# Two scans of 512 columns joined into one of 1024 in a Mamba-style decoder layer, with the first column of the second state corrected ahead of the scan

## The chip, the cores and the metric

The kernel runs on one core of one Trainium2 chip. A core has four compute engines with a queue of instructions each: PE (TensorE, matmuls; PEld are its weight loads), DVE (VectorE), ACT (ScalarE) and POOL (GpSimd). SP (SyncE) only issues DMAs here. The engines run side by side and wait for one another by semaphores. The metric is the device time of one execution in microseconds (us). The kernel before takes 3095.3 us, the median of three runs (3093.15 to 3097.14).

## The reference, cut to what matters

One decoder layer on x of 2 sequences x 2048 tokens x 512 features, float32: a selective scan (Mamba), a cross attention, a feed-forward part, each followed by a layer norm. The change concerns the selective scan alone:

```
xz = x @ W_in + b_in;  u = silu(first half);  z = second half       # 1024 channels each
B, C = split(u @ W_xproj + b_xproj)                                 # 16 states each
dt = softplus(u @ W_dt + b_dt);  A = -exp(A_log)                    # A: 1024 x 16
for t in time:                                                      # separately per sequence
    h = h * exp(dt[t] * A) + (dt[t] * u[t]) * B[t]                  # h: 1024 x 16
    y[t] = sum over states(h * C[t]) + D * u[t]
out = (y * silu(z)) @ W_out + b_out
```

For one channel and one state this is a recurrence over time, h = decay * h + input. VectorE has an instruction for it, which runs along the columns of a row and takes the value before the first column as a separate operand.

## The kernel before, in words

`selective_scan_phase` fills about the first 1925 us, `attention_ffn_phase`, which the change leaves alone, the rest. The scan phase cuts the 4096 tokens into 8 chunks of 512 (`TS`), four per sequence; the 1024 channels into 8 tiles of 128; and a tile with its 16 states into 8 pairs. A row on the 128 partitions is 8 channels x 16 states of one group, so a pair is two such groups (`o` = 0 and 1) and there are 8 x 8 x 8 = 512 pairs. Each engine goes through the pairs in the same order; what it does in the turn of one pair is called a slot here, and slots count from 0 to 63 within a chunk.

For one pair: PE spreads dt over the states into `r_ps` (`rep_dt`, L400, two banks of 512 columns, twice two matmuls) and dt*u into `u_ps` (`rep_dtu`, L413). ACT makes the decays in place, two `Exp` (`exps`, L642). DVE multiplies `u_ps` by B into the buffer `h` (`dbu`, L786), and scans each of the two rows of `h` with its bank of `r_ps` (`scans`, L799, two instructions), starting from `carry` where the chunk continues a sequence and from zero in chunks 0 and 4. ACT saves the last column of both rows (`save_carry`, L648). POOL multiplies by C (`weigh`, L903), and PE sums over the states into `y_ps` (L429). Per tile, DVE gates y (`gate`, L805) and ACT scales u by D (`skip`, L653).

`r_ps` holds two pairs. So `rep_dt(pair + 2)` waits for the scans of `pair`; after it come `exps(pair + 2)` on ACT, then the scans of `pair + 2` on DVE, which has `dbu(pair + 2)`, the scans of `pair + 1` and `dbu(pair + 3)` to do in between. That is the loop in which the change lies. `s_scan`, `s_da` and `s_m1` count scans, decays and `dbu`.

Beside that, in the slots of chunk n the engines make u, z and dt of chunk n + 1, by a written table (`Plan`): which slots hold which projection on PE, where ACT splits the next x into two float16 parts (`x_high`, `Plan.x`, and `x_low` on POOL, L870), and when the silu of u and z and the softplus of dt run on ACT. A silu brings two loads of an activation table. There are eight silu in a chunk's slots, each of two tiles. In the last chunk the projection by W_out begins from slot 24 on (`OUTS`); its weights are split into float16 parts in slots 15 to 23 (`w_out_high`, `w_out_scaled` on ACT, `w_out_low` on DVE, L810, and on POOL, L925).

SP issues all loads and stores in one order (`step(c, j)`: one call for each chunk and tile), so whatever it waits for holds back what stands behind it.

Of the kernel before, what the change touches and what calls it, by code (L numbers as in the profile page):

```python
# [9 lines left out]
ALU = mybir.AluOpType  # L10
# [45 lines left out]
W_OUT_LOW_AT = (19, 20, 22, 23)  # L56
# [6 lines left out]
class Plan:  # L63
    def __init__(self, n):
# [13 lines left out]
        start = 31 if n == 1 else 26  # L78
        self.x = {1: (25, 28), 2: (20, 23)}.get(n, (19, 23))
        self.u_high = (start + 8, start + 16)  # L80
        at, places = start, {}
        for name in self.order:
            long = name in ("dt3", "dt4", "dt5", "dt6", "dt7") and 2 <= n < NC - 1
# [37 lines left out]
def selective_scan_phase(nc, a):  # L121

    with ExitStack() as ctx:
# [38 lines left out]
        c_rep = sb("c_rep", [P, 2, TS])  # L162
        h = sb("h", [P, H_GROUPS, 4, TS])
# [18 lines left out]
        s_hl = sem("a_last_hc_ready")  # L182
        s_hc, s_sum, s_y, s_skip = sem("a_hc_ready"), sem("a_summed"), sem("a_y_ready"), sem("a_skip_ready")
# [3 lines left out]
        s_wor, s_woh, s_wos, s_wol, s_wod = (sem(f"a_w_out_{n}") for n in ("loaded", "high", "scaled", "low", "first_low"))  # L187
# [25 lines left out]
        x_stages = (x_t, soft)  # L213

        def place(pair):
            return pair // PAIRS, pair % PAIRS // 8, pair % 8

        @block.sync
        def _(sp):
            def load_x(n, part, stage):  # L220
# [83 lines left out]
            def step(c, j):  # L304
                more = c + 1 < NC
                if j == 6 and more:
                    store_z(c + 1, 0)
                load_u(c, j)
                load_z(c, j)
# [8 lines left out]
                if more:  # L318
# [8 lines left out]
                    if j == 7:  # L327
                        store_z(c + 1, 1)

            def load_y_tile(i):  # L330
                g = i % 4
                if i < 2:
                    sp.wait_ge(s_wod, i + 1)
                elif i < 4:
                    sp.wait_ge(s_wol, 2 * i - 2)
# [53 lines left out]
        def _(pe):  # L389
            def rep_dt(pair):  # L390
# [11 lines left out]
                last.then_inc(s_rep, 1)  # L402

# [68 lines left out]

            def out_piece(i, s):
                out = OUTS[i]
                k0, k1 = out.pieces[s]
                if s == out.first:
                    if i == 0:
                        pe.wait_ge(s_ev, pieces_before(NC))
                        pe.wait_ge(s_wod, 2)
# [3 lines left out]
                else:  # L483
                    if i == 0 and k0 == 3:
                        pe.wait_ge(s_wol, 4)
# [34 lines left out]
            for w in range(2):  # L520
                spread_state(first, w, r_ps[:, 2 + w, :])
            rep_dt(0)
            rep_dtu(0)
            pe.wait_ge(s_ev, first.index("C") + 1)
            rep_dt(1)
            rep_dtu(1)
            for pair in range(TOTAL):
# [4 lines left out]
                s = pair - (NC - 1) * PAIRS  # L532
                for i in range(OUT_TILES):
# [10 lines left out]
        def _(act):  # L544
# [64 lines left out]
            def evacuate_dt(plan, t, src=pj[:, :]):  # L609
                g = plan.n * NJ + t  # L610
                act.wait_ge(s_pj, plan.index(f"dt{t}") + 1)
# [24 lines left out]
            def exps(pair):  # L636
                c, j, p = place(pair)
                act.wait_ge(s_rep, pair + 1)
                for o in range(2):
                    col = j * NSTATE + 2 * p + o  # L640
                    bank = r_ps[:, 2 * (pair % 2) + o, :]
                    nc.scalar.activation(bank, bank, ACT.Exp, scale=decay[:, col:col + 1]).then_inc(s_da, 1)  # L642

            def save_carry(pair):
                c, j, p = place(pair)
                act.wait_ge(s_scan, 2 * pair + 2)
# [43 lines left out]

            def w_out_scaled(q):
                act.wait_ge(s_woh, q + 1)
                rows = slice(2 * q, 2 * q + 2)
                nc.scalar.activation(w_out_raw[:, rows, :], w_out_raw[:, rows, :], ACT.Copy, scale=W_SCALE).then_inc(s_wos, 1)
# [52 lines left out]
            for pair in range(TOTAL):  # L747
# [7 lines left out]
                if pair + 2 < TOTAL:  # L755
                    exps(pair + 2)
                if pair % 8 == 3:
# [1368 lines left out]
```

## Time and profile before

| | us |
|---|---|
| median of three runs | 3095.3 |
| the profiled execution's own time | 3097.61 |
| its span, first to last instruction | 3095.9 |
| DVE busy | 2697.2 |
| PE busy | 2835.3 |
| ACT busy | 2008.8 |
| POOL busy | 1827.0 |

The share of busy time mixes two phases; the scan phase is read from windows inside it. The chain that ended last could not be followed far back in this profile: its named parts add up to less than half the span, nearly all of them in the second phase. For the scan phase it is the idle time of DVE, and what ended it, that says what bounds.

### The profile page before, as it was taken

How to read it: one execution, taken by the hardware profiler on the slowest of the kernel's cores; microseconds unless marked ns; L12 is line 12 of the kernel's file. 1: busy time of each engine (PE TensorE's matmuls, PEld its weight loads, DVE VectorE, ACT ScalarE, POOL GpSimd, SP SyncE). 2: the span in 40 equal slices, each digit the busy share in tenths (PEclk: the TensorE clock that was granted, in tenths of full speed). 3: DMA queues.
4: the chain of work that ended last, by engine and by line, in shares of the span. 5: the costliest groups of instructions: out<-in, count | busy, mean ns of one | idle time of the engine just before them, and what ended most of it. 6: DMA issues, size and time to landing. Idle time of an engine off the chain costs nothing. (4 is left out here: it accounts for less than half of the span.)

```text
span 3095.9 us, 48996 instructions
## 1 busy us (share of the span) xinstructions
PE 2835.3 (92%) x18940; PEld 1263.5 (41%) x18940; DVE 2697.2 (87%) x3072; ACT 2008.8 (65%) x3600; POOL 1827.0 (59%) x940
## 2 busy tenths in 40 slices
PE   7988989889889889889899898899999999999998
PEld 2222222222222222222222223566666767667665
DVE  6999999999999999999999988776666777777775
ACT  6777776676776776776777644555555555655565
POOL 4887988888888888888988987312211111111100
PEclk9999999999999999999999899899999999999999
DMA  4112111111111121111122233701111000010000
GB/s 162 52 52 70 42 56 61 52 52 56 52 57 56 46 65 53 41 65 53 42 65 80 87 96 119 233 29 43 43 43 46 33 23 23 23 37 29 23 8 15
DMA packets 123897, 176.65 MB, mean 57 GB/s; under 512 B 15154, under 2 KB 50610, under 8 KB 123156
## 3 DMA queue, kind: packets, MB, share of 16 engines
q1 hardware_dynamic: 123668, 173.51, 17.3%
q8 instruction: 155, 2.54, 0.3%
q14 instruction: 74, 0.61, 0.1%
HBM read 104.33 MB, written 67.04 MB: 55 GB/s over the span
## 5 line engine op out<-in xcount | busy, mean ns | idle before, releaser
L903 POOL TENSOR_TENSOR h<-h,c_rep 128x1024 f32<-128x1024 f32 x511 | 1197.9, 2359 | 242.2 <-ACT carry L648 241.1
L799 DVE TENSOR_TENSOR_SCAN h<-r_ps,carry,h 128x512 f32<-128x512 f32 x768 | 938.6, 1262 | 5.5 <-ACT r_ps L642 5.4
L642 ACT ACTIVATE r_ps<-r_ps,decay 128x512 f32<-128x512 f32 x1024 | 631.8, 656 | 330.1 <-PE r_ps L400 330.0
L786 DVE TENSOR_TENSOR h<-u_ps,b_rep 128x1024 f32<-128x1024 f32 x512 | 612.9, 1197 | 21.7 <-PE u_ps L413 21.6
L413 PE MATMUL u_ps<-dtu,spread 32*128 32x512 f16 x2048 | 313.6, 383 | 115.1 <-DVE h L786 113.5
L400 PE MATMUL r_ps<-dt,spread 32*128 32x512 f16 x2048 | 312.8, 381 | 44.5 <-DVE h L799 44.3
L1989 POOL TENSOR_TENSOR o_in<-o_in,rows 128x1024 f32<-128x1024 f32 x15 | 37.0, 2464 | 487.7 <-DMA o_in<-o_dram 487.7
L799 DVE TENSOR_TENSOR_SCAN h<-r_ps,zero,h 128x512 f32<-128x512 f32 x256 | 312.8, 1261 | 3.6 <-ACT r_ps L642 3.6
L429 PE MATMUL y_ps<-h,gather 128*32 128x512 f32 x2048 | 285.1, 624 | 0.0
L40 PE MATMUL fps<-x,region 128*128 128x256 f16 x1024 | 280.5, 274 | 3.0 <-issue 2.4
L42 PE MATMUL fps<-x,region 128*128 128x256 f16 x1024 | 280.1, 274 | 0.0
L41 PE MATMUL fps<-x,region 128*128 128x256 f16 x1024 | 280.0, 273 | 0.0
L40 PE MATMUL pj<-x_high,region 128*128 128x512 f16 x484 | 190.5, 394 | 41.7 <-POOL x_low L870 18.8
L400 PEld LDWEIGHTS r_ps<-dt,spread 32*128 32x128 f16 x2048 | 59.0, 92 | 378.0 <-DVE h L799 220.8
L2007 POOL TENSOR_TENSOR y<-y_t,y 128x1024 f16<-128x1024 f32 x13 | 29.2, 2248 | 299.1 <-ACT y L1505 299.1
L40 PE MATMUL nat<-region,act 128*128 128x512 f16 x512 | 194.4, 380 | 4.2 <-DVE act L1776 4.2
L40 PE MATMUL pj<-u_high,region 128*128 128x512 f16 x504 | 196.3, 389 | 2.0 <-ACT zs L587 1.3
L41 PE MATMUL pj<-u_low,region 128*128 128x512 f16 x504 | 194.4, 386 | 0.0
L42 PE MATMUL pj<-u_high,region 128*128 128x512 f16 x504 | 194.4, 386 | 0.0
L41 PE MATMUL nat<-region,act 128*128 128x512 f16 x512 | 194.2, 379 | 0.0
L42 PE MATMUL nat<-region,act 128*128 128x512 f16 x512 | 194.2, 379 | 0.0
L42 PE MATMUL pj<-x_high,region 128*128 128x512 f16 x484 | 189.0, 390 | 0.0
(257 smaller groups left out, 5599.3 us busy)
## 6 DMA issues: line engine op xcount, KB each, us to landing
u_t_dram<-u SPq DMA_DIRECT2D x16, 1024.0 KB, 5.1
uz<-u_t_dram SPq DMA_DIRECT2D x64, 256.0 KB, 3.8
z_t_dram<-zs SPq DMA_DIRECT2D x32, 512.0 KB, 3.0
uz<-z_t_dram SPq DMA_DIRECT2D x64, 256.0 KB, 3.6
y_t_dram<-uz SPq DMA_DIRECT2D x64, 256.0 KB, 2.1
region<-y_t_dram SPq DMA_DIRECT2D x32, 256.0 KB, 3.5
result<-x SPq DMA_DIRECT2D x16, 512.0 KB, 2.8
x_t<-dram_x_t SPq DMA_DIRECT2D x15, 512.0 KB, 4.3
```

The source lines that it names most:

```text
L40: nc.tensor.matmul(out, w[0], x[0], start=start, stop=False)
L41: nc.tensor.matmul(out, w[0], x[1], start=False, stop=False)
L42: return nc.tensor.matmul(out, w[1], x[0], start=False, stop=stop)
L400: last = nc.tensor.matmul(r_ps[:, 2 * (pair % 2) + o, :], spread[32 * i:32 * i + 32, p // 2, :], dt16[32 * i:32 * i + 32, s, j, :], start= ...
L413: last = nc.tensor.matmul(u_ps[:, o, :], spread[32 * i:32 * i + 32, p // 2, :], dtu16[32 * i:32 * i + 32, s, j, :], start=(s == 0), stop=( ...
L429: last = nc.tensor.matmul(y_ps[32 * i:32 * i + 32, :], gather[:, q, :], h[:, g % H_GROUPS, i, :], start=(q == 0), stop=(q == 3))
L642: nc.scalar.activation(bank, bank, ACT.Exp, scale=decay[:, col:col + 1]).then_inc(s_da, 1)
L786: nc.vector.tensor_tensor(h[:, g % H_GROUPS, o:o + 2, :], u_ps[:, :, :], b_rep[:, c % 2:c % 2 + 1, :].broadcast_to([P, 2, TS]), ALU.mult). ...
L799: nc.vector.tensor_tensor_scan(row, r_ps[:, 2 * (pair % 2) + o, :], row, start, ALU.mult, ALU.add)\
L903: nc.gpsimd.tensor_tensor(rows, rows, c_rep[:, c % 2:c % 2 + 1, :].broadcast_to([P, 2, TS]), ALU.mult)\
L1989: nc.gpsimd.tensor_tensor(o_in[:, :, :], o_in[:, :, :], row(0), ALU.add).then_inc(s_ob, 1)
L2007: nc.gpsimd.tensor_tensor(y16[:, 1, :, t * P:(t + 1) * P], y_first[i % 2] if i < Y_PAIRED else y_t[:, :, :], y16[:, 0, :, t * P:(t + 1) * ...
```

## The change

Where a chunk continues a sequence, the second row of a pair is now scanned behind the first in the same instruction, 1024 columns from one start. For this the decay in the first column of the second row must be zero, so that nothing runs over from the first row, and what the recurrence would have added there, decay * carry, must already stand in that column of `h`.

- The first columns of banks 1 and 3 of `r_ps` are set to zero once (`joint_decay_zero`). After that `rep_dt` and `exps` leave them out for `o` = 1: 511 columns instead of 512.
- The missing decay is worked out apart. For each tile, SP stores the first column of dt (128 numbers) to DRAM and, once that has landed, loads it back spread over the states (`joint_dt`); POOL multiplies by A (`joint_dt_scaled`), ACT takes `Exp` (`joint_decay`), 8 decays per partition for the 8 pairs.
- For each pair ACT adds decay * carry to the first column of the second row (`joint_column`), after `dbu` of that pair and its `exps`. The scan waits for both `Exp` and for this column.
- All this is done in the six chunks that continue a sequence (1 to 3, 5 to 7); in chunks 0 and 4 the start is zero and only the joined scan is new.
- `evacuate_dt` on ACT also waits until the first column of the tile two before has been stored.
- `Plan`: the production for chunk 1 starts at slot 32 instead of 31, for chunk 2 at 27 instead of 26, with x one slot later for chunk 2; dt3 for chunk 2 takes 3 slots instead of 4. PE waits for the two halves of the split x apart, each where it needs it.
- `step` on SP loads u and z before it stores z, where it did it behind.
- Last chunk: DVE makes all four low parts of W_out (slots 17 to 20), where it made two and POOL the other four half-size pieces after two scalings on ACT. PE runs 6 more matmuls, whose result nobody reads, in each of the slots 21, 22 and 23 (`keep_awake`).

```diff
-        start = 31 if n == 1 else 26
-        self.x = {1: (25, 28), 2: (20, 23)}.get(n, (19, 23))
+        start = {1: 32, 2: 27}.get(n, 26)
+        self.x = {1: (25, 28), 2: (21, 24)}.get(n, (19, 23))
...
+            def joint_dt(n, t):
+                if n >= NC or not continued(n):
+                    return
+                done = joints_before(n) * NJ + t
+                sp.wait_ge(s_dt, n * NJ + t + 1)
+                sp.dma_start(a["dt_first"][n, t, :].rearrange("(c r) -> r c", c=8),
+                             dt[:, (n * NJ + t) % 2, 0:1], allow_slow_non_contiguous=True).then_inc(s_jst, 16)
+                sp.wait_ge(s_jst, 16 * (done + 1))
...
+                sp.dma_start(joint[:, t, :, :, :].rearrange("p h o q -> p (h o q)"), a["dt_first"][n, t, :].rearrange("(c r) -> c r", c=8).unsqueeze(1)
+                             .broadcast_to([8, NSTATE, 16])).then_inc(s_jld[t % 2], 16)
...
-                    pe.wait_ge(s_scan, 2 * pair - 2)
+                    pe.wait_ge(s_scan, pair - 1)
...
-                        last = nc.tensor.matmul(r_ps[:, 2 * (pair % 2) + o, :], spread[32 * i:32 * i + 32, p // 2, :],
-                                                dt16[32 * i:32 * i + 32, s, j, :], start=(s == 0), stop=(s == 1))
+                        last = nc.tensor.matmul(r_ps[:, 2 * (pair % 2) + o, o:TS], spread[32 * i:32 * i + 32, p // 2, :],
+                                                dt16[32 * i:32 * i + 32, s, j, o:TS], start=(s == 0), stop=(s == 1))
...
-                        if s == plan.u[0][0]:
-                            pe.wait_ge(s_xl, 2 * n + 2)
+                        if t == 0:
+                            pe.wait_ge(s_xl, 2 * n + 1 + plan.u[0].index(s))
...
+            def keep_awake():
+                pe.wait_ge(s_ev, pieces_before(NC))
+                for k in range(6):
+                    nc.tensor.matmul(pj[:, :], w_out[0][:, 0, 0:P], w_out[0][:, 0, :], start=True, stop=True)
...
-                    bank = r_ps[:, 2 * (pair % 2) + o, :]
+                    bank = r_ps[:, 2 * (pair % 2) + o, o:TS]
                     nc.scalar.activation(bank, bank, ACT.Exp, scale=decay[:, col:col + 1]).then_inc(s_da, 1)
...
+            def joint_column(pair):
+                c, j, p = place(pair)
+                if continued(c):
+                    if p == 0:
+                        act.wait_ge(s_jexp, joints_before(c) * NJ + j + 1)
+                    act.wait_ge(s_m1, pair + 1)
+                    act.wait_ge(s_carry, pair - PAIRS + 1)
+                    col = j * NSTATE + 2 * p + 1
+                    at = h[:, pair // 2 % H_GROUPS, 2 * (pair % 2) + 1, 0:1]
+                    nc.scalar.activation(at, joint[:, j, p % 2, 1, p // 2:p // 2 + 1], ACT.Identity, bias=at, scale=carry[:, col:col + 1])\
+                        .then_inc(s_joint, 1)
...
                 if pair + 2 < TOTAL:
+                    joint_decay(pair + 2)
                     exps(pair + 2)
+                    joint_column(pair + 2)
...
-                for o in range(2):
-                    col = j * NSTATE + 2 * p + o
-                    dve.wait_ge(s_da, 2 * pair + o + 1)
-                    row = h[:, pair // 2 % H_GROUPS, 2 * (pair % 2) + o, :]
-                    start = carry[:, col:col + 1] if c % PER_SEQ else zero[:, 0:1]
-                    nc.vector.tensor_tensor_scan(row, r_ps[:, 2 * (pair % 2) + o, :], row, start, ALU.mult, ALU.add)\
-                        .then_inc(s_scan, 1)
+                dve.wait_ge(s_da, 2 * pair + 2)
+                if continued(c):
+                    dve.wait_ge(s_joint, joints_before(c) * PAIRS + pair % PAIRS + 1)
+                o = 2 * (pair % 2)
+                col = j * NSTATE + 2 * p
+                rows = h[:, pair // 2 % H_GROUPS, o:o + 2, :].rearrange("p o t -> p (o t)")
+                start = carry[:, col:col + 1] if continued(c) else zero[:, 0:1]
+                nc.vector.tensor_tensor_scan(rows, r_ps[:, o:o + 2, :].rearrange("p o t -> p (o t)"), rows, start,
+                                             ALU.mult, ALU.add).then_inc(s_scan, 1)
...
-                if W_OUT_AT + 2 <= s < W_OUT_AT + 4:
+                if W_OUT_AT + 2 <= s < W_OUT_AT + 6:
                     w_out_low(s - W_OUT_AT - 2)
```

ACT's queue in chunk 3, slots 6 and 7 at the start of tile 1's decays (`carry` begins a slot's work on the loop; L592 is the silu of z with its table loads, L633 and L634 split dt), before:

```order
955 L587 ACTIVATE zs<-pj,b_in 128x512 [waits a_projected]
956 L648 ACTIVATE carry<-h 128x2 [waits a_scanned]
957 L642 ACTIVATE r_ps<-r_ps,decay 128x512 [waits a_dt_spread]
958 L642 ACTIVATE r_ps<-r_ps,decay 128x512
959 L592 ACT_TABLE_LOAD
960 L592 ACTIVATE zs<-zs 128x1024 [waits a_evacuated]
961 L546 ACT_TABLE_LOAD
962 L648 ACTIVATE carry<-h 128x2 [waits a_scanned]
963 L642 ACTIVATE r_ps<-r_ps,decay 128x512 [waits a_dt_spread]
964 L642 ACTIVATE r_ps<-r_ps,decay 128x512
```

and now, at the same place (L721 is `save_carry`, L697 `exps`, L714 `joint_column`, L703 `joint_decay`, L644 the silu):

```order
1108 L721 ACTIVATE carry<-h 128x2 [waits a_scanned]
1109 L697 ACTIVATE r_ps<-r_ps,decay 128x512 [waits a_dt_spread]
1110 L697 ACTIVATE r_ps<-r_ps,decay 128x511
1111 L714 ACTIVATE h<-joint,h,carry 128x1 [waits a_carry_saved,a_dbu_ready]
1112 L644 ACT_TABLE_LOAD
1113 L644 ACTIVATE zs<-zs 128x1024 [waits a_evacuated]
1114 L598 ACT_TABLE_LOAD
1115 L721 ACTIVATE carry<-h 128x2 [waits a_scanned]
1116 L703 ACTIVATE joint<-joint 128x2x4 [waits a_joint_dt_scaled]
1117 L697 ACTIVATE r_ps<-r_ps,decay 128x512 [waits a_dt_spread]
1118 L697 ACTIVATE r_ps<-r_ps,decay 128x511
1119 L714 ACTIVATE h<-joint,h,carry 128x1 [waits a_carry_saved,a_dbu_ready,a_joint_decay_ready]
```

The `Exp` stay where they were; behind each pair's two stands a column of one element per partition, and ahead of a tile's first pair the small `Exp` of its eight decays.

DVE's queue in the last chunk, slots 16 to 19 (L810 is `w_out_low`), before:

```order
1002 L786 TENSOR_TENSOR h<-u_ps,b_rep 128x1024
1003 L799 SCALAR_TENSOR_TENSOR h<-r_ps,carry,h 128x512 x2
1004 L810 SCALAR_TENSOR_TENSOR region<-region 128x2x512
1005 L786 TENSOR_TENSOR h<-u_ps,b_rep 128x1024
1006 L799 SCALAR_TENSOR_TENSOR h<-r_ps,carry,h 128x512 x2
1007 L810 SCALAR_TENSOR_TENSOR region<-region 128x2x512
1008 L786 TENSOR_TENSOR h<-u_ps,b_rep 128x1024
1009 L799 SCALAR_TENSOR_TENSOR h<-r_ps,carry,h 128x512 x2
1010 L786 TENSOR_TENSOR h<-u_ps,b_rep 128x1024
1011 L799 SCALAR_TENSOR_TENSOR h<-r_ps,carry,h 128x512 x2
1012 L805 TENSOR_TENSOR uz<-y_ps,uz 128x512
```

and now (L854 is `dbu`, L869 the scan, L880 `w_out_low`, L875 the gate):

```order
1002 L854 TENSOR_TENSOR h<-u_ps,b_rep 128x1024
1003 L869 SCALAR_TENSOR_TENSOR h<-r_ps,carry,h 128x1024
1004 L880 SCALAR_TENSOR_TENSOR region<-region 128x2x512
1005 L854 TENSOR_TENSOR h<-u_ps,b_rep 128x1024
1006 L869 SCALAR_TENSOR_TENSOR h<-r_ps,carry,h 128x1024
1007 L880 SCALAR_TENSOR_TENSOR region<-region 128x2x512
1008 L854 TENSOR_TENSOR h<-u_ps,b_rep 128x1024
1009 L869 SCALAR_TENSOR_TENSOR h<-r_ps,carry,h 128x1024
1010 L880 SCALAR_TENSOR_TENSOR region<-region 128x2x512
1011 L854 TENSOR_TENSOR h<-u_ps,b_rep 128x1024
1012 L869 SCALAR_TENSOR_TENSOR h<-r_ps,carry,h 128x1024
1013 L880 SCALAR_TENSOR_TENSOR region<-region 128x2x512
```

Two rows of scans of 512 columns became one of 1024, and two more `w_out_low` stand between the pairs.

## Rows read from the trace of the kernel before

**Rows 1.** The page's first line.

```profile
span 3095.9 us, 48996 instructions
```

**Rows 2.** Windows: stretch, its length, busy us (instructions) per engine, PE clock, DMA share, GB/s.

```profile
1000.00:1200.00 200.00, 177.57 (x1043) 48.88 (x1043) 199.40 (x176) 144.29 (x259) 173.78 (x89) 0.98 0.17 52
```

**Rows 3.** DVE's waits in chunk 4 (987 to 1215 us): total us, times, longest.

```profile
DVE h L799 <- ACT r_ps L642: 0.6, 1, 0.6
```

**Rows 4.** Groups of 400 to 1700 us: form, count, busy us, mean ns, idle before, releaser.

```profile
L799 DVE TENSOR_TENSOR_SCAN h<-r_ps,carry,h 128x512 f32<-128x512 f32 x600 | 733.3, 1262 | 4.3 <-ACT r_ps L642 4.3
L642 ACT ACTIVATE r_ps<-r_ps,decay 128x512 f32<-128x512 f32 x729 | 449.7, 655 | 202.7 <-PE r_ps L400 202.7
L786 DVE TENSOR_TENSOR h<-u_ps,b_rep 128x1024 f32<-128x1024 f32 x364 | 435.4, 1196 | 4.0 <-PE u_ps L413 4.0
...
L805 DVE TENSOR_TENSOR uz<-y_ps,uz 128x512 f32<-128x512 f32 x46 | 30.4, 660 | 0.0
```

**Rows 5.** Timeline, chunk 3, ACT and DVE around three silu: start, us, what, [idle].

```profile
781.16 1.24 ACT L642 ACTIVATE r_ps<-r_ps,decay 128x512 f32<-128x512 f32 x2 [1.61 <-PE r_ps L400]
...
782.42 1.28 ACT L592 ACT_TABLE_LOAD   x1
782.77 2.44 DVE L799 TENSOR_TENSOR_SCAN h<-r_ps,carry,h 128x512 f32<-128x512 f32 x2
...
785.14 1.20 DVE L786 TENSOR_TENSOR h<-u_ps,b_rep 128x1024 f32<-128x1024 f32 x1
...
786.08 0.20 ACT L648 ACTIVATE carry<-h 128x2 f32<-128x2 f32 x1
786.19 1.22 ACT L642 ACTIVATE r_ps<-r_ps,decay 128x512 f32<-128x512 f32 x2
...
786.96 2.46 DVE L799 TENSOR_TENSOR_SCAN h<-r_ps,carry,h 128x512 f32<-128x512 f32 x2 [0.63 <-ACT r_ps L642]
...
827.65 1.22 ACT L642 ACTIVATE r_ps<-r_ps,decay 128x512 f32<-128x512 f32 x2
...
829.35 2.44 DVE L799 TENSOR_TENSOR_SCAN h<-r_ps,carry,h 128x512 f32<-128x512 f32 x2
...
975.43 1.22 ACT L642 ACTIVATE r_ps<-r_ps,decay 128x512 f32<-128x512 f32 x2
976.33 2.44 DVE L799 TENSOR_TENSOR_SCAN h<-r_ps,carry,h 128x512 f32<-128x512 f32 x2
```

**Rows 6.** DVE's waits in the last chunk (1673 to 1930 us).

```profile
DVE h L786 <- PE u_ps L413: 9.4, 9, 4.6
DVE region L817 <- PE pj L496: 7.0, 2, 4.5
```

**Rows 7.** DMA issues: count, KB each, median us from issue to landing.

```profile
bc_dram<-bc SPq DMA_DIRECT2D x7, 64.0 KB, 1.9
```

**Rows 8.** Timeline, PE before the first u of chunk 1 and of chunk 2.

```profile
179.12 0.61 PE L40 MATMUL pj<-x_high,region 128*128 128x512 f16 x1 [5.71 <-POOL x_low L870]
...
396.26 0.61 PE L40 MATMUL pj<-x_high,region 128*128 128x512 f16 x1 [5.39 <-POOL x_low L870]
```

**Rows 9.** DVE's waits in chunk 0 (57 to 297), then in chunk 1 (297 to 530).

```profile
DVE h L786 <- PE u_ps L413: 6.7, 4, 5.6
...
DVE h L786 <- PE u_ps L413: 3.8, 1, 3.8
```

**Rows 10.** Timeline, last chunk: `w_out_low` on DVE, a POOL one, PE's first output tile.

```profile
1735.99 2.94 DVE L810 SCALAR_TENSOR_TENSOR region<-region 128x1024 f16<-128x1024 f32 x1
...
1737.81 2.14 POOL L890 TENSOR_TENSOR dt<-dt 128x512 f16<-128x512 f32 x1
...
1742.36 2.10 DVE L810 SCALAR_TENSOR_TENSOR region<-region 128x1024 f16<-128x1024 f32 x1
...
1760.14 1.16 POOL L890 TENSOR_TENSOR dt<-dt 128x512 f16<-128x512 f32 x1
...
1769.66 0.58 PE L40 MATMUL pj<-region,u_high 128*128 128x512 f16 x1 [3.61 <-POOL u_low L931]
```

More of the change, by code:

```diff
@@ L82, in __init__ @@
         for name in self.order:
-            long = name in ("dt3", "dt4", "dt5", "dt6", "dt7") and 2 <= n < NC - 1
+            long = name in ("dt4", "dt5", "dt6", "dt7") and 2 <= n < NC - 1 or name == "dt3" and 3 <= n < NC - 1
             count = 2 if name[0] in "uz" else 4 if long else 3
@@ L186, in selective_scan_phase @@
         s_yout = [sem("a_y_stored_even"), sem("a_y_stored_odd")]
-        s_wor, s_woh, s_wos, s_wol, s_wod = (sem(f"a_w_out_{n}") for n in ("loaded", "high", "scaled", "low", "first_low"))
+        s_wor, s_woh, s_wol = (sem(f"a_w_out_{n}") for n in ("loaded", "high", "low"))
         s_bcst, s_brep, s_crep = sem("a_bc_stored"), sem("a_b_replicated"), sem("a_c_replicated")
@@ L305, in step @@
                 more = c + 1 < NC
+                load_u(c, j)
+                load_z(c, j)
+                if j == 7:
+                    joint_dt(c + 1, 0)
+                if j == 1:
+                    joint_dt(c, 3)
+                if j == 2 and c == 1:
+                    joint_dt(c, 4)
                 if j == 6 and more:
                     store_z(c + 1, 0)
-                load_u(c, j)
-                load_z(c, j)
                 if j == 0 and more:
@@ L328, in step @@
                         store_z(c + 1, 1)
+                        joint_dt(c + 1, 1)
+                if j == 0:
+                    joint_dt(c, 2)
+                if j == 1 and c != 1:
+                    joint_dt(c, 4)
+                if j == 2:
+                    joint_dt(c, 5)
+                if j == 3:
+                    joint_dt(c, 6)
+                    joint_dt(c, 7)
             def load_y_tile(i):
                 g = i % 4
[L332 to L335, printed above, removed]
+                if i < 4:
+                    sp.wait_ge(s_wol, i + 1)
                 else:
@@ L532, in _ @@
                 s = pair - (NC - 1) * PAIRS
+                if PLANS[-1].dt[-1][-1] - PAIRS < s < OUT_AT:
+                    if s == PLANS[-1].dt[-1][-1] - PAIRS + 1:
+                        pe.wait_ge(s_woh, 1)
+                    keep_awake()
                 for i in range(OUT_TILES):
@@ L904, in weigh, with joint_dt_scaled @@
                     .then_inc(s_hc, 1)
+            def joint_dt_scaled(pair):
+                c, j, p = place(pair)
+                if continued(c) and p == 0:
+                    pool.wait_ge(s_jld[j % 2], 16 * ((joints_before(c) * NJ + j) // 2 + 1))
+                    odd = decay[:, j * NSTATE:(j + 1) * NSTATE].rearrange("p (q h o) -> p h q o", q=QUADS, h=2)[:, :, :, 1]
+                    nc.gpsimd.tensor_tensor(joint[:, j, :, 1, :], joint[:, j, :, 1, :], odd, ALU.mult).then_inc(s_jmul, 1)
             def produce(plan, s):
@@ L966, in _ @@
                     weigh(pair)
+                if pair + 5 < TOTAL:
+                    joint_dt_scaled(pair + 5)
                 for plan, s in producing(pair):
@@ L969, in _ @@
                 s = pair - (NC - 1) * PAIRS
-                if s in W_OUT_LOW_AT:
-                    w_out_low(4 + W_OUT_LOW_AT.index(s))
                 for i in range(OUT_TILES):
```

46 lines of the change are left out of this document (30 added, 16 removed).

## The prediction

> **What bounds the kernel now.** I read the page first: the span is 3095.9 us [rows 1], the execution's own time 3097.6, 2.3 above the median of the runs, so a sum made on this profile is taken off the median. Then the windows. In a window in the middle of the scan phase DVE is busy 199.4 of 200 us, PE 177.6, POOL 173.8, ACT 144.3, and PE's granted clock is 0.98 [rows 2]. DVE's own waits say the same: in the whole of chunk 4, 228 us long, it waited 0.6 us, once, for ACT [rows 3]. So away from its ends the phase is DVE's queue, and whatever shortens that queue shortens the phase until another engine hands over too late. The reader should keep both halves: DVE has no idle time, and ACT, which hands it the decays, has 28% of slack on average but not in every slot.
>
> **The joined scan.** It removes 512 starts of an instruction. What one start costs I take from two ordinary DVE operations: 512 columns last 660 ns, 1024 columns 1196 [rows 4], so 512 more columns cost 536 and 124 are fixed. A scan of 512 columns lasts 1262; if it takes twice as long per column it spends 2 x 536 = 1072 on columns and 190 on the rest, and one of 1024 would last 2144 + 190 = 2334 ns. The two of before last 2.44 us from the first's start to the second's end [rows 5]. The gain is 0.107 us per pair. The bounds: nothing, if all of the 1262 grows with the columns; 0.19, if the whole rest is saved and none of it overlapped before. I take 0.107, since the count of two per column fits the plain operations' slope. On DVE's path lie 448 pairs of chunks 0 to 6 and 24 of chunk 7: 472 x 0.107 = 50.5 us. In the last 40 pairs the output projection shares PE and DVE already waits for PE [rows 6]; I count half, 2 us. Together 52.5 off.
>
> The Trainium skill ("Perfetto Trace Analysis", Optimizing Scalar/DVE Operations) gives a VectorE instruction on PSUM some 125 ns of overhead and advises larger operations on a saturated engine; by that estimate the term would be 59 us instead of 50.5. The same section says that breaking up instructions can let work be done sooner where an engine holds up others; that is the other side of this change, and the next term.
>
> **What the scan now waits for.** Before, the first scan needed the first `Exp` only: where ACT is late it began 0.13 us after that one's end (786.96, against 786.19 and half of the two) [rows 5]. Now it needs both, and in six chunks a column behind them. A small ACT operation: `save_carry` lasts 0.20 and the next starts 0.11 after it (786.08, 786.19) [rows 5]. The next operation starts about 0.09 before the second `Exp` ends (two of 655 ns in 1.22 us) [rows 4, 5], so the column is ready 0.11 after that end and the scan can begin 0.24 after it; without a column 0.13. Each earlier column also puts ACT 0.11 back. On the other side DVE comes sooner, by 0.107 per scan it did since.
>
> Most pairs have room: ACT has the decays well before DVE comes. It has none behind a silu, whose table loads hold ACT from 782.42 to 786.08, longer than a pair [rows 5]. Eight silu stand in a chunk's slots. Three kinds, all shown [rows 5]:
> - DVE waits already (786.96, idle 0.63). The second `Exp` ends at 787.41, the scan could begin at 787.76 (0.24, and 0.11 of the column before): 0.80 later than now. DVE would have come 0.21 earlier (two scans), which the first term has counted as won. Loss 1.0. There are one or two of these in a chunk; I take two.
> - The five others: `Exp` end 828.87, scan at 829.35. Ready at 829.22, DVE there at 829.14: loss 0.1.
> - Behind a gate: `Exp` end 976.65, scan 976.33. Ready 977.00, DVE there at 976.12: loss 0.9. One per chunk.
> That is 2.0 + 0.5 + 0.9 = 3.4 per chunk, 20 us in six chunks. The `Exp` of eight decays ahead of a tile's first pair, another 0.11, falls on four of these silu: 2.5 us more. In chunks 0 and 4, without columns, 0.79 x 2 + 0.66 = 2.2 each, 4.5. In all 27 us back. Bounds: 10 if only the pairs that wait today lose and the others catch up; 60 if a column is ready 0.5 us later than I reckon, since then all eight silu pairs lose it too (8 x 0.5 x 6 = 24) and pairs with a slack of near 1 us begin to.
>
> **SP, DRAM and POOL.** 48 times SP stores 128 numbers, waits for the landing and loads them. A store of this kind lands in 1.9 us [rows 7], so each holds SP for some 2.5 us, and the value is there some 5 us after dt. The calls stand one to two pairs behind the slot in which dt is made, and POOL wants the value in slot -5 of the tile: 2 pairs of margin for tile 0, over 4 for the rest; in chunk 1 POOL will wait for tile 0's once, some 3 us, and POOL has 26 us in 200 to spare [rows 2]. I count nothing; bound 5 us. If that cover went, POOL's products would come late for PE's sums, then DVE for buffer space.
>
> **The wait for x.** In chunks 0 and 1 PE waited 5.71 and 5.39 us for the second half of the split x [rows 8], and DVE then 5.6 and 3.8 for PE [rows 9]. Now the first projection starts a slot later and its first half needs only the first half of x; a slot is 3.5 us and the second half another, so the wait is gone but for a rest that DVE doesn't see. 9 off; bounds 5 and 9.4.
>
> **The last chunk.** DVE gets two more `w_out_low`: 2.10 us alone, 2.94 where POOL works beside it [rows 10]: 4 to 6 us added. Off go DVE's waits of 4.6 for the first output tile, which PE began 3.61 late because POOL was late, and at half clock [rows 10], and parts of the 7.0 at the first two tiles' ends [rows 6]: POOL is relieved of its `w_out_low`, and `keep_awake` fills PE's idle slots ahead. I take 8 of these 11.6; the ends of the tiles stay on the path. Net 3 off; bounds 4 on, 8 off.
>
> On the two added `w_out_low` the Trainium skill ("SBUF — State Buffer", Who interferes with whom) says that a VectorE instruction with two inputs in SBUF contends with GpSimd's reads. The rows bear it out: beside the L810 of 2.94 us a POOL operation of 1.16 took 2.14 [rows 10]. By that rule both new ones cost 2.9 and POOL 1 us each; by the short row 2.1. I took the middle.
>
> **Sum.** -52.5 + 27 - 9 - 3 = -37.5. From the median, 3095.3 - 37.5 = 3057.8; I say 3057.
>
> **Rivals.**
> 1. The handover becomes the loop. Place: between `exps` on ACT and DVE's scan. If the column reaches DVE 1.2 us after the second `Exp` and not 0.24, the eight silu pairs of a chunk lose 0.96 more and six with a slack of near 1 us some 0.4: 10 us per chunk, 60 in six. 3057 + 60 = 3117, slower. It decides from about 0.85 us on, where the loss eats the 37.5. For it: ACT's bursts are longer than a pair. Against it: a small ACT operation lasts 0.20 [rows 5].
> 2. The joined scan saves nothing, every ns of it growing with the columns. Then DVE also comes no earlier and the second term falls to some 18: 3095.3 + 18 - 12 = 3101. For it: nothing in the trace shows a scan of another length. Against it: 190 ns would be hard to spread over columns that cost twice the plain 536.
> 3. The losses behind the silu are smaller, since a pair that is late gives ACT, PE and POOL time, and PE's clock falls less; the last chunk gains its 8: 3095.3 - 52.5 + 10 - 9 - 8 = 3036.
>
> **Chances.** Forecast (3040 to 3075) 0.58; rival 3 (below 3040) 0.17; between forecast and no change (3075 to 3089) 0.08; rival 1 0.10, of which 0.08 slower and 0.02 no change; rival 2 0.07, half no change, half slower. About 6 us, 0.2%, is what a measurement tells from no change. Faster 0.83, same 0.06, slower 0.11. The range 3030 to 3090 leaves out most of rivals 1 and 2 and the low tail of rival 3, under 0.2 together.
>
> **What the profile after would show.** The scan's row: 512 of them, near 2334 ns; much above 2400 and rival 2 holds. DVE's waits for ACT in a chunk: near 4 us, on some eight pairs, all behind a silu; over 10 and it is rival 1. The column's row near 200 ns. No wait for `x_low` of over 2 us. DVE's waits for PE and for the output tiles in the last chunk: some 8 us instead of 16. Wrong would be: DVE waiting for a loaded dt or POOL's product, a slower matmul of 511 columns, or a span of the second phase that differs.

## The result and the profile after

The changed kernel takes 3122.2 us (median of five runs, 3113.6 to 3124.0) against 3096.6 of before on the same chip: a ratio of 1.0074, 95% interval 1.0062 to 1.0086. It is 26 us slower by the medians, 23 by the ratio; 3057 was forecast. Two of its five runs took 3113.6 and 3113.7, three 3122.2 to 3124.0, so a difference to after is known to some 5 us. The profiled execution is one of 3122.2 us with a span of 3120.2.

The page of after, its first line and the rows of the scan: line, engine, form and count, then busy us and mean ns of one, then the idle time before them and what ended most of it.

```profile
span 3120.2 us, 49910 instructions
...
L869 DVE TENSOR_TENSOR_SCAN h<-r_ps,carry,h 128x1024 f32<-128x1024 f32 x384 | 900.4, 2345 | 54.8 <-ACT h L714 35.2
...
L869 DVE TENSOR_TENSOR_SCAN h<-r_ps,zero,h 128x1024 f32<-128x1024 f32 x128 | 300.9, 2351 | 12.7 <-ACT r_ps L697 12.5
```

The joined scan lasts 2345 ns where 2334 were worked out, against 2.44 us for the two of [rows 5]. But 54.8 us of waiting stand before those of the six continued chunks. The page puts 35.2 down to the column (L714), and 18.7 more, in the row below, to `save_carry` (L721), which stands behind it:

```profile
DVE h L869 <- ACT carry L721: 18.7, 21, 3.3
```

These were waits for the column too: all 21 of these scans start 0.13 us after a column's end, as 52 of the 54 behind L714 do. Two rows say what the column and the decays' `Exp` last (min, median, max in ns), and one how long a store of dt's first column takes to land (count, KB, us):

```profile
L714 ACT ACTIVATE h<-joint,h,carry x384: 377/383/419, 303.1 to 1940.6; 128x1 f32<-128x1 f32 x192
L703 ACT ACTIVATE joint<-joint x48: 191/193/226, 301.9 to 1912.2; 128x8 f32<-128x8 f32 x48
```

```profile
dt_first_dram<-dt SPq DMA_DIRECT2D x48, 0.5 KB, 7.0
```

The column is 383 ns long, not 200, and the store lands after 7.0 us, not after the 1.9 of [rows 7]. Behind a silu of chunk 5 the timeline of after shows the handover (start, length, what, idle before):

```profile
1337.85 1.28 ACT L598 ACT_TABLE_LOAD   x1
1339.14 0.20 ACT L721 ACTIVATE carry<-h 128x2 f32<-128x2 f32 x1
...
1339.25 0.20 ACT L703 ACTIVATE joint<-joint 128x8 f32<-128x8 f32 x1
1339.35 1.22 ACT L697 ACTIVATE r_ps<-r_ps,decay 128x512 f32<-128x512 f32 x2
1340.49 0.38 ACT L714 ACTIVATE h<-joint,h,carry 128x1 f32<-128x1 f32 x1
1340.77 0.68 ACT L616 ACTIVATE u<-pj,b_in 128x512 f32<-128x512 f32 x1
1341.00 2.35 DVE L869 TENSOR_TENSOR_SCAN h<-r_ps,carry,h 128x1024 f32<-128x1024 f32 x1 [0.60 <-ACT h L714]
```

The second `Exp` ends at 1340.57, the column 0.30 later, the scan starts 0.13 after that: 0.43 instead of 0.24. The operation behind the column starts 0.28 after it, so each earlier column puts ACT back by 0.28, not by 0.11. DVE's waits in the whole of chunk 5 of after, to be held against [rows 3]:

```profile
DVE h L869 <- ACT h L714: 5.9, 9, 1.5
DVE h L869 <- ACT carry L721: 2.2, 2, 1.8
DVE h L854 <- PE u_ps L456: 0.4, 1, 0.4
```

8.5 us, where some 4 were foreseen. SP's waits (total, times, longest) over the scan phase, and the boundary of chunks 0 and 1:

```profile
SPq L242 <- DMA dt_first_dram<-dt: 304.2, 48, 10.7
```

```profile
282.67 0.64 SPq L235 DMA_DIRECT2D dt_first_dram<-dt  x1
...
288.96 0.71 SPq L242 DMA_DIRECT2D joint<-dt_first_dram  x1
...
292.14 0.21 POOL L981 TENSOR_TENSOR joint<-joint,decay 128x8 f32<-128x8 f32 x1 [5.83 <-DMA joint<-dt_first_dram]
...
296.92 1.03 PE L456 MATMUL u_ps<-dtu,spread 32*128 32x512 f16 x4 [6.26 <-POOL dtu L961]
297.99 1.23 DVE L854 TENSOR_TENSOR h<-u_ps,b_rep 128x1024 f32<-128x1024 f32 x1 [5.95 <-PE u_ps L456]
```

Here is the chain that was counted at nothing: store, landing, load, GpSimd's product 5.83 late; behind it in GpSimd's queue stand dt's low parts, PE gets them 6.26 late, DVE stops for 5.95. PE's clock suffers as well. First 10 us of after that hold this stop, then the same 10 us of the run without transfers below, which has no such stop (stretch, length, PE, PEld, DVE, ACT, POOL busy, PEclk, DMA share, GB/s):

```profile
290.00:300.00 10.00, 3.74 (x18) 0.97 (x14) 4.05 (x3) 1.24 (x2) 7.03 (x5) 0.61 0.08 27
```

```profile
290.00:300.00 10.00, 9.56 (x63) 2.89 (x63) 9.71 (x7) 8.56 (x20) 9.06 (x5) 1.00 0.00 0
```

PE stood idle from 290.7 to 296.9 and then worked at the lower of its two levels (1.2 GHz): a matmul of 512 columns took 0.61 us there and 0.38 before, and the granted clock was 0.61 in the mean of the stretch.

### The profile page after: what moved, and what is told of

Same layout as the page of the kernel before. It is cut to its first block and busy times, and to the rows that moved or that the text cites. A ratio compares the mean times of both kernels' runs of the same rounds, so it can differ in the third digit from the quotient of the medians.

```text
span 3120.2 us, 49910 instructions
## 1 busy us (share of the span) xinstructions
PE 2838.1 (91%) x18960; PEld 1267.9 (41%) x18960; DVE 2656.0 (85%) x2562; ACT 2109.9 (68%) x4030; POOL 1830.8 (59%) x984
## 2 busy tenths in 40 slices
DMA packets 137345, 177.13 MB, mean 57 GB/s; under 512 B 28595, under 2 KB 64051, under 8 KB 136597
## 5 line engine op out<-in xcount | busy, mean ns | idle before, releaser
L869 DVE TENSOR_TENSOR_SCAN h<-r_ps,carry,h 128x1024 f32<-128x1024 f32 x384 | 900.4, 2345 | 54.8 <-ACT h L714 35.2
L697 ACT ACTIVATE r_ps<-r_ps,decay 128x512 f32<-128x512 f32 (+1 forms) x1024 | 631.2, 656 | 296.4 <-PE r_ps L439 293.2
L854 DVE TENSOR_TENSOR h<-u_ps,b_rep 128x1024 f32<-128x1024 f32 x512 | 617.8, 1207 | 29.4 <-PE u_ps L456 29.2
L439 PE MATMUL r_ps<-dt,spread 32*128 32x511 f16 (+1 forms) x2048 | 317.6, 386 | 47.3 <-DVE h L869 47.0
L869 DVE TENSOR_TENSOR_SCAN h<-r_ps,zero,h 128x1024 f32<-128x1024 f32 x128 | 300.9, 2351 | 12.7 <-ACT r_ps L697 12.5
L40 PE MATMUL pj<-x_high,region 128*128 128x512 f16 x484 | 194.1, 401 | 44.8 <-ACT u L616 21.5
L40 PE MATMUL pj<-u_high,region 128*128 128x512 f16 x504 | 200.8, 398 | 4.9 <-ACT zs L639 4.7
L42 PE MATMUL pj<-u_high,region 128*128 128x512 f16 x504 | 199.0, 395 | 0.0
L42 PE MATMUL pj<-x_high,region 128*128 128x512 f16 x484 | 193.0, 399 | 0.0
```

The lines of the kernel that those rows point to most:

```text
L40: nc.tensor.matmul(out, w[0], x[0], start=start, stop=False)
L42: return nc.tensor.matmul(out, w[1], x[0], start=False, stop=stop)
L439: last = nc.tensor.matmul(r_ps[:, 2 * (pair % 2) + o, o:TS], spread[32 * i:32 * i + 32, p // 2, :], dt16[32 * i:32 * i + 32, s, j, o:TS], ...
L854: nc.vector.tensor_tensor(h[:, g % H_GROUPS, o:o + 2, :], u_ps[:, :, :], b_rep[:, c % 2:c % 2 + 1, :].broadcast_to([P, 2, TS]), ALU.mult). ...
L869: nc.vector.tensor_tensor_scan(rows, r_ps[:, o:o + 2, :].rearrange("p o t -> p (o t)"), rows, start, ALU.mult, ALU.add).then_inc(s_scan, 1)
```

## The experiments

All times are medians. The runs a, b with d, c, and e with f are four sets, each on another chip, and before beside them is 3095.3 to 3097.2; a difference between sets holds to some 2 us more. The ratio is to before, with its interval. The last column is read from the profiled execution: us from the first product (`dbu`) of chunk 2 to that of chunk 7. It leaves out both ends of the scan phase and the second phase, and it varies little: in before, a4, e1 and e2, whose scans there are the same, it is 1142.7 to 1143.4.

| run | what it is | us | ratio | chunks 2 to 6 |
|---|---|---|---|---|
| before | | | | 1143.4 |
| after | the change | 3122.2 | 1.0074 [1.0062, 1.0086] | 1146.7 |
| a1_no_column | after, no column | 3093.4 | 0.9995 [0.9985, 1.0005] | 1126.0 |
| a2_no_dram | after, no transfers of dt | 3105.9 | 1.0038 [1.0024, 1.0051] | 1146.9 |
| a3_neither | after, neither | 3063.6 | 0.9903 [0.9888, 0.9918] | 1118.7 |
| a4_sides | all but the joined scan | 3092.5 | 0.9989 [0.9980, 0.9998] | 1143.3 |
| b1_split | after, store and load apart | 3108.4 | 1.0035 [1.0023, 1.0047] | 1147.2 |
| b2_between | b1, column between the `Exp` | 3109.6 | 1.0035 [1.0022, 1.0049] | 1150.2 |
| b3_scaled | b2, one operand less | 3098.5 | 1.0005 [0.9996, 1.0015] | 1141.1 |
| d1_dummy | a3, column that nobody waits for | 3087.9 | 0.9970 [0.9960, 0.9980] | 1133.9 |
| c1_late2 | two scans in two pairs behind silu | 3086.3 | 0.9973 [0.9964, 0.9982] | 1127.5 |
| c2_late1 | in one pair | 3083.1 | 0.9957 [0.9944, 0.9970] | 1128.7 |
| c3_late2_two | c1, the column's first form | 3087.5 | 0.9970 [0.9959, 0.9981] | 1125.2 |
| c4_starts | joined in chunks 0 and 4 only | 3087.7 | 0.9975 [0.9966, 0.9985] | 1136.6 |
| e1_x_only | before, x wait alone | 3094.5 | 0.9990 [0.9979, 1.0000] | 1142.7 |
| e2_last_only | before, last chunk alone | 3096.3 | 0.9998 [0.9990, 1.0007] | 1142.8 |
| f1_middle | best mixture | 3072.3 | 0.9915 [0.9902, 0.9928] | 1125.7 |
| f2_middle1 | f1, one pair behind silu | 3081.1 | 0.9944 [0.9931, 0.9956] | 1129.5 |

**What costs: column, transfers, or both.** Theory A was the column on ACT, theory B that each store holds SP and what loads behind it. The edits in short:

```diff
a1:  -joint_column(pair + 2)              # and the scan's wait for it
a2:  -joint_dt(n, t)                      # store and load on SP; joint is zero
a3:  -both, GpSimd's product and the Exp of the decays
a4:  -both and the joined scan
```

> The kernel after without the column operation on ScalarE and the scan's wait for it; the second row's carry from the chunk before is left out, all else stays (the stores and loads of dt's first column, GpSimd's products, the Exp of the decays). If the column is what costs (theory A: 0.38 us of ScalarE per pair, and the scan's start 0.43 instead of 0.24 us behind the second Exp): about 3080 us, 42 below after. If the store of dt's first column that holds SyncE is the larger loss (theory B): within 10 us of after, about 3112.

> The kernel after without the stores and loads of dt's first column on SyncE; GpSimd's products, the Exp and the column stay and work on zeros, so the carry's decay is wrong. Theory B (SyncE held 10.7 us by each of 48 stores, late loads behind it): 15 to 20 us below after, about 3104. Theory A alone (the column): within 4 us of after.

> The kernel after without both: no column, no store or load, no product, no Exp of the decays; the second row's carry is left out. What is left is the joined scan and the edits that the kernel's other part made. Both theories together: about 3060 us, 35 below before. If the two losses overlap (a stall of one hides one of the other): less than the sum of the two runs before, about 3070.

> The kernel before with all edits except the joined scan and what it needs: the Plan's places, the wait for half of x_low, the order of SyncE's loads, w_out's low part on VectorE and the extra matmuls in the last chunk. The prediction's terms for these are -9 (x wait) and -3 (last chunk): 3084 us. Rival: the plan's moves give back what the x wait saves, 3095 us.

Measured: without the column 28.8 us less, without transfers 16.3 less, without both 58.5 less. Both theories hold, and each loss is larger where the other is gone: the column alone costs 3105.9 - 3063.6 = 42.2, the transfers alone 3093.4 - 3063.6 = 29.8. Each of these two holds the 48 `Exp` of the decays and GpSimd's 48 products as well, which a3 leaves out. They add up to 72.0 and cost 58.5 together: 13.5 us are lost as soon as either is there. (The 10.7 us that the expectation of a2 gives each store is the longest of SP's 48 waits; the mean is 6.3.) DVE's waits in chunk 5 of the run without transfers are those of after to the tenth; the run with neither has 3.7 us left:

```profile
DVE h L862 <- ACT r_ps L694: 2.4, 2, 1.5
DVE h L862 <- ACT carry L718: 1.1, 1, 1.1
DVE h L849 <- PE u_ps L455: 0.2, 1, 0.2
```

The side edits gave 3 us instead of 12.

The last column says where each loss lies. The column costs 28.2 of its 42.2 in chunks 2 to 6 (a2 against a3). The transfers cost nothing there beside the column, though 32 of the 48 stores stand there (after 1146.7, a2 1146.9); without the column they cost 7.3 (a1 against a3). What they cost in after lies at the ends: the stop at the boundary of chunks 0 and 1, and one in the last chunk, where loads of y for the output projection (L378) stood behind such a store and load:

```profile
1797.83 0.55 SPq L235 DMA_DIRECT2D dt_first_dram<-dt  x1
1804.51 0.60 SPq L242 DMA_DIRECT2D joint<-dt_first_dram  x1
1805.17 2.10 SPq L378 DMA_DIRECT2D region<-y_t_dram  x4
...
1810.41 1.06 ACT L771 ACTIVATE u_high<-region 128x1024 f16<-128x1024 f32 x1 [8.35 <-DMA region<-y_t_dram]
...
1813.11 2.35 DVE L869 TENSOR_TENSOR_SCAN h<-r_ps,carry,h 128x1024 f32<-128x1024 f32 x1 [3.34 <-ACT carry L721]
1819.08 1.23 DVE L854 TENSOR_TENSOR h<-u_ps,b_rep 128x1024 f32<-128x1024 f32 x1 [3.62 <-PE u_ps L456]
```

Neither stop is in a2. A further 4.1 us between the two profiles stand ahead of the first store (282.67): slot 60 of chunk 0 begins at 277.88 in after and at 273.75 in a2. No transfer made these, so the pair of profiles gives the transfers 12 us and not 16.

**What about the column costs: ACT's time or the longer handover.** Theory occupancy is the first, theory latency the second. b1 sets store and load apart and leaves chunk 1's first three tiles with two scans; b2 moves the column; b3, made from b2, multiplies the carry by its decay on GpSimd, eight pairs at once, so that the column adds one per-partition operand instead of multiplying by one and adding another; d1 takes the kernel with neither and lets ACT do a column that nobody waits for.

```diff
b1:  -store; wait; load                   +store; other transfers; wait; load
b2:  -Exp, Exp, column                    +Exp, column, Exp
b3:  -activation(at, decay, Identity, bias=at, scale=carry)
     +activation(at, at, Identity, bias=scaled_carry)
d1:  +activation(scratch, joint, Identity, bias=d_skip, scale=decay)
```

> The kernel after with SyncE's store of dt's first column and its load set apart, so that SyncE does other transfers while the store lands, and with two scans of 512 in the first three tiles of chunk 1, whose loads came late. If the 16 us that the run without stores and loads won are SyncE's holds and the late loads: about 3106 us, as without any transfer, or 2 to 4 less for the 24 pairs of chunk 1 that have no column. If they are something else that the transfers do (their packets, ScalarE's waits for the stores): about 3115 to 3120.

> The run before (store and load apart) with one thing more: ScalarE does the column between the pair's two Exp instead of behind them. ScalarE's work stays the same; what goes is the column's place at the end of the handover (scan 0.43 us behind the second Exp plus 0.1). If the handover's length makes the stalls (theory latency): 15 to 25 us less than the run before. If it is ScalarE's occupancy (0.28 us per pair behind each Silu): at most 6 us less. A loss would come from the column waiting there for VectorE's product.

> The run before with the carry already multiplied by its decay: GpSimd does one product of 128x8 more per eight pairs, and ScalarE's column is an addition with one operand per partition (bias) instead of two (scale and bias). If the second operand makes the column 0.38 us long: it becomes about 0.25 us, ScalarE's pitch 0.2, and the time falls 3 to 8 us below the run before. If not: the column stays at 0.38 us and the time within 2 us of it.

> The kernel without column, stores and loads (3064 us), plus an operation of the column's form on ScalarE at the column's place in the 384 continued pairs, that writes a scratch column and that nothing waits for; the second row's carry is left out. It measures ScalarE's occupancy without the handover. The run with column and without transfers was 42 us above the one with neither. Theory occupancy: most of it comes back, 3095 to 3106 us. Theory latency (the scan's wait behind the column): 3064 to 3075 us.

b1 came to 3108.4, near the run without transfers, though it makes 45 of the 48 stores: the loss is the late loads and what they hold up, not the packets. It takes 24 columns away as well, and SP still waits 124.4 us for landings, 24 times; which of its two edits gave how much was not tried apart.

b2 changed nothing. By its expectation that speaks for theory occupancy, but it parts the theories less than it was meant to: the scan now waits for a second `Exp` that comes as much later. d1 parts them. It came to 3087.9, between its two forecasts: 24.2 us of the column's 42.2 (21 by the ratios; 15.2 of 28.2 in chunks 2 to 6) come from ACT's time alone. The other 18.0 stand for the scan's wait behind the column and for the decays' `Exp` and products, which d1 leaves out too. Neither theory holds alone. DVE's waits for the `Exp` in chunk 5 of b2, then of d1, where it was 2.4 in a3:

```profile
DVE h L902 <- ACT r_ps L723: 6.0, 9, 1.5
...
DVE h L871 <- ACT r_ps L694: 6.8, 8, 1.8
```

b3 won 11 us, more than the 3 to 8 expected. Its column's row:

```profile
L743 ACT ACTIVATE h<-h,joint x258: 277/283/323, 539.0 to 1679.6; 128x1 f32<-128x1 f32 x129
...
  POOL joint L1025: 10.3, 11
```

283 ns with one operand read per partition, 383 with two, 193 for the decays' `Exp` of eight columns with none: some 95 ns an operand. The Trainium skill ("ScalarE: Activation LUTs", What ACT_TABLE_LOAD costs) has this: 186 ns fixed with immediate scale and bias and about 93 for each per-partition pointer. The rows agree, and the prediction would have had the column's length from it. The second line is ACT waiting for GpSimd's new product, 10 us that c1 and c2 removed by asking for it one pair earlier; their column stands behind the second `Exp` again.

**Where the column may stand.** Joined scans everywhere but behind a silu (two pairs each in c1 and c3, one in c2; c3 with the first form of the column, that is b1 with fewer columns), or only where no column is needed (c4).

```diff
-joined for every pair
+c1: not in q + 2, q + 3 for a silu in slot q    +c2: not in q + 3
+c4: chunks 0 and 4 only
```

> The run with the scaled carry (3098.5 us), but with two scans of 512 and no column in the two pairs behind each Silu on ScalarE (80 of the continued pairs more, 280 columns are left), and the carry's product on GpSimd one pair earlier, for which ScalarE waited 10 us. If ScalarE's lateness behind the Silu is where the column costs: per continued chunk some 6.5 us of stalls fall to about 1.5, against 16 times 0.107 us of the joined scan given back, six times 3.2 us, and 5 us of the wait for GpSimd: about 3075 us, clearly below before. If the column costs everywhere alike: 3098.5 less 80 columns of 384, about 3090.

> As the run before, but two scans only in the one pair behind each Silu (320 columns are left). By the theory of ScalarE's lateness the pair just before the late one also counts, since its column stands ahead of the Silu: 2 to 6 us above the run before, about 3079 us. If only the late pair's own handover counts: 3 us below it, about 3072.

> Two scans in the two pairs behind each Silu, but with the column in its first form (scale and bias, behind the second Exp, no product of the carry on GpSimd). If the column costs only where ScalarE is late, its form no longer matters: within 4 us of the run with the scaled carry, about 3077. If its 0.1 us more count in all 280 pairs: 8 us or more above it.

> The run with the other edits alone (3092.5 us), with the joined scan only in chunks 0 and 4, which begin a sequence and need no column, no store, no load. By the traces of the run with neither, the joined scan is worth 4.3 us in chunk 0 and 6.7 us in chunk 4: 3081 us. If the joined scan's gain shows only where all chunks have it: 3090 us or more.

All four beat before, by 8 to 13 us. c1 missed its 3075 by 11 us and came nearer to its rival's 3090, c4 missed its 3081 by 7, and c2 lies below c1, not above. c1, c2 and c3 are hardly better than c4, which has no column at all.

Chunks 2 to 6 show more than the medians. There c1, c2 and c3 take 1125.2 to 1128.7 us, 15 to 18 below before, 8 to 11 below c4 and as long as after without any column (a1, 1126.0). So the joined scan pays in the continued chunks once the column is kept from the silu, and the column's form no longer matters (c3 1125.2, c1 1127.5). What c1 to c3 lose against that lies outside these chunks.

**The two side terms, and the best mixture.** e1 and e2 are before with one side edit each. f1 joins chunks 0 and 4, and 2, 3, 5, 6 as c1 does, with two scans in chunks 1 and 7, where ACT and SP have most else to do; f2 the same with c2's rule.

> The kernel before with only the edits of the x wait: the Plan's places, the first u matmuls' wait for half of x_low, and the order of SyncE's loads. By the prediction's term: 9 us below before, about 3087. If the next thing is late in its place (the profile of all side edits has 3.6 us on VectorE in chunk 1 at the same place, and four waits of about a microsecond more in chunk 0): within 3 us of before.

> The kernel before with only the edits of the last chunk: w_out's low part on VectorE in four products, the extra matmuls that keep TensorE busy, the waits that go with them. By the prediction's term: 3 us below before, about 3093. If the extra VectorE products cost what the saved wait gives: the same as before within 2 us.

> Joined scan in chunks 0 and 4 without column, and in chunks 2, 3, 5 and 6 with the scaled carry outside the two pairs behind each Silu; chunks 1 and 7 as before with two scans. Against the run that joins only chunks 0 and 4 (3087.7 us) the traces give 2 to 2.6 us per chunk of the four: about 3079 us, the fastest version that computes all. If the column's cost stays hidden elsewhere (PE, the clock): 3086 to 3090.

> As the run before, with two scans only in the one pair behind each Silu. In the traces of the two kernels with all continued chunks this lost 0.5 to 1.6 us per chunk against two pairs, though the time was 3 us better: 3079 to 3083 us.

e2 is before's time. e1 is 1.8 us below before, and its interval reaches 1. A row of before in chunk 0, then e1's waits in chunk 0 and in chunk 1, against [rows 9]:

```profile
DVE h L799 <- ACT r_ps L642: 3.0, 4, 1.1
...
DVE h L799 <- ACT r_ps L642: 6.1, 7, 1.2
DVE h L786 <- PE u_ps L413: 1.1, 3, 0.7
...
DVE h L786 <- PE u_ps L413: 2.6, 3, 2.2
DVE h L799 <- ACT r_ps L642: 0.5, 1, 0.5
```

In this profile, of an execution of 3089.3 us, the 5.6 are gone and 3.1 us of waits for `Exp` have come; in chunk 1 the 3.8 became 2.6. Its twelve runs lie between 3086.4 and 3101.0: of the six with a mean granted clock of PE of 0.979 or more, five lie below 3091, and the six with less lie above 3093. So the term seems to be there in some executions and lost in others; what decides the clock there was not tried.

f1 is the fastest version that computes all: 3072.3 us, 24 below before and 50 below after. Its profile is of its slowest run, 3082.4 us. DVE's waits in its chunk 5:

```profile
DVE h L898 <- ACT r_ps L727: 2.1, 4, 1.4
DVE h L906 <- ACT h L744: 0.2, 1, 0.2
```

2.3 instead of 8.5, with the scan joined in 48 of 64 pairs. f2 stands 9 us above f1 by the medians and 3.8 in chunks 2 to 6. The column that stands ahead of the silu, which one pair's two scans don't cover, would explain the 3.8; this is argued and not shown, and c2 against c1 goes the other way by the medians (-3.2) and 1.2 the same way in these chunks.

## Why the prediction was wrong

- **The joined scan, -52.5, and its wait for the second `Exp`: right, though 6 us too large.** Without columns the prediction's own numbers give -52.5 + 8 x 2.2 = -34.9. Measured, a3 against a4: -28.8. The pitch of a pair where DVE doesn't wait fell from 3.481 to 3.372 us, 0.109 against the 0.107 of the sum. Rival 2 is out. The estimate of 59 us that the prediction made from the Trainium skill ("Perfetto Trace Analysis", Optimizing Scalar/DVE Operations) was farther off than the one from rows: 472 times 0.109 is 51.4.
- **The column: this step failed.** "A small ACT operation: `save_carry` lasts 0.20 and the next starts 0.11 after it" was taken for the column. `save_carry` has no operand per partition, the column has two: 0.38 and 0.28. The sum had 27 - 17.6 = 9 us for columns and decays; the columns cost 29 in after, columns, decays and products 42 without the transfers. The second fault is in the working: it counted late pairs only. d1 shows that 24 of the 42 us come though nothing waits for the column: ACT, with its bursts, has no room for 384 x 0.28 = 108 us at the places where it is late anyway. This was rival 1, with its place right and its price wrong: not 1.2 us behind the `Exp`, but 0.43, and ACT's own time with it. That its 3117 lies near 3122 is luck in part, since it had nothing for the transfers.
- **SP, DRAM and POOL, 0 with a bound of 5: failed.** The 1.9 us of [rows 7] are a store of 32 rows of 2 KB; this one writes 128 single numbers. It lands after 7.0 us, and loads that came late behind such holds of SP stopped POOL, PE and DVE at the boundary of chunks 0 and 1, and ACT and DVE in the last chunk: 16 us in after (12 by the profiles), 30 alone. POOL's wait was foreseen as 3 us and was 5.83; that dt's low parts, next in POOL's queue, would then hold PE and DVE was not foreseen. The Trainium skill ("DMA: Bandwidth & Descriptors", Rules for kernel authors) says that such a pattern becomes one descriptor per element; that speaks against the step, though the page has no time for it. The rows agree: after has 28595 packets under 512 B and before 15154, which is 280 more for each store with its load.
- **The x wait, -9: mostly not there.** e1: -1.8. The wait for `x_low` went; in the profile other waits took a part of its place.
- **The last chunk, -3: not there.** e2: -0.1. Its waits in e2 fell from [rows 6] as below, by 3.2 us and not by 8, and the two added `w_out_low` took 2.4 of them back:

```profile
DVE region L878 <- PE pj L541: 8.3, 2, 4.9
DVE h L847 <- PE u_ps L455: 4.9, 5, 2.0
```

```profile
1747.81 1.19 DVE L871 SCALAR_TENSOR_TENSOR region<-region 128x1024 f16<-128x1024 f32 x1
...
1752.43 1.19 DVE L871 SCALAR_TENSOR_TENSOR region<-region 128x1024 f16<-128x1024 f32 x1
```

The prediction's 4 to 6 us for these two rested on a misread row: the L810 of 2.10 us in [rows 10] was not alone, as POOL's two products from 1741.03 to 1746.66 ran beside it. With nothing of POOL beside it (1752.43) the same operation takes 1.19.

Of the other signs, the scans' row came as foreseen, and no wait for `x_low` is left. The last chunk's did not: DVE's waits for PE and the output tiles are 17.7 us in after, where 8 were foreseen and [rows 6] have 16.4:

```profile
DVE h L854 <- PE u_ps L456: 12.3, 9, 3.6
...
DVE region L887 <- PE pj L542: 5.4, 2, 3.1
```

Three signs of being wrong came in part: DVE's stop behind POOL's product; a second phase 3.2 us longer (1176.6 against 1173.4); and the decays' matmuls, 386 ns in the mean against 381, though with the 511 columns of a3 they take 383. In sum: -28.8 (joined scan) + 58.5 (column and transfers) - 2.8 (side edits) = +26.9 on 3095.3, which gives 3122.2. This comes out by construction, as the pieces are differences of neighbouring runs.

Left open: why by the medians c1 to c3 lie 0 to 5 us below c4 and f1 15. In chunks 2 to 6, c1, c3 and f1 are within 2.3 us of each other, so it is outside them. Only chunks 1 and 7 differ between the kernels of c1 and f1; they were not tried one by one. The profiles can't tell: those of c1 and f1 are both of runs of 3082.4 us, near c1's fastest and f1's slowest. Part of the scatter is the second phase, which no edit touches: 1173.4 us at a granted clock of 0.99 in before, 1185.8 at 0.98 in c3.

## What to carry to other kernels

An operation of one column is not priced by its size: count its per-partition operands, and count it on its engine's queue in every slot, not only where someone waits for it. Before moving work to an engine with "slack on average", look whether the slack lies in the same slots as the bursts; taking the work away from those slots (c3 against b1, 20.9 us by the medians, two chips) was worth more here than shortening it (b3 against b2, 11.1). A small transfer is not priced by its bytes: look at how many pieces it has. The queue that waits for its landing holds everything behind it, but that costs only where something behind it is needed soon, here at a chunk's boundary and in the last chunk, so look there first and put other transfers between store and load. Where executions of one kernel differ by 10 us, compare a stretch in the middle, where equal kernels agree, before comparing totals.

## What the hardware showed that was not expected

- A store of 128 single numbers from 128 partitions, 0.5 KB, took 7.0 us to land in the median; one of 64 KB in rows took 1.9 [rows 7].
- Each per-partition operand makes a small ACT operation some 95 ns longer (193, 283, 383).
- A stop of PE at the boundary of chunks 0 and 1 was followed by the lower of its two clock levels (1.2 GHz) in the same stretch (0.61 in the mean of 10 us against 1.00).
- Executions of one kernel differ with PE's granted clock: e1 from 3086.4 us at 0.982 to 3101.0 at 0.976. A term of under 10 us can't be read from the total of one profile.
- The same operation (`w_out_low`, two operands in SBUF) took DVE 1.19 us with nothing of POOL beside it and 2.10 to 2.96 where a POOL product had begun before it (e2). Where DVE's began first, at 1747.81, it took 1.19 and POOL's took 2.23 instead of 1.28.
